# Output projection of the last unit placed before the other unit's MLP, with row shifts by small matrix products, in a one-core Perceiver-style kernel

## What is computed

```python
x = x + cross_attention(ctx, layernorm(x), mask)     # 16 heads of 64, keys from ctx
x = x + causal_attention(layernorm(x))               # one head of 256
x = x + ffn(layernorm(x))                            # two layers, below
```

```python
h = shift_token(x)                                   # right half of the features: from the row above
q, k, v = split(h @ wqkv)                            # 8 heads of 64
q, k = rotary(l2norm(q) * qs), rotary(l2norm(k) * ks)
x = x + local_attention(q, k, v) @ wo                # window of 128
h = layernorm(shift_token(x)) * lg + lb              # shift again, then mean and variance by row
a, g = split(h @ w1 + b1)
x = x + (a * gelu(g)) @ w2 + b2                      # hidden width 682
```

## Time and profile before

| | us |
|---|---|
| median of 3 runs | 1082.38 |
| lowest, highest | 1081.82, 1087.89 |
| the profiled execution | 1083.38 |
| its span in the profile | 1081.6 |

### The profile page before, as it was taken

One profiled execution on the slowest core, in us unless ns is written; L12 is line 12 of the kernel. 1 busy time (PEld: TensorE's weight loads), 2 busy tenths in 40 slices (PEclk: granted clock), 3 DMA queues, 4 the chain that ended last, 5 costly groups with the idle time before them and its releaser, 6 DMA issues. The chain is left out here.

```text
span 1081.6 us, 25643 instructions
## 1 busy us (share of the span) xinstructions
PE 1020.2 (94%) x8664; PEld 947.2 (88%) x8665; DVE 822.5 (76%) x3037; ACT 659.4 (61%) x1532; POOL 203.0 (19%) x260
## 2 busy tenths in 40 slices
PE   3899999999999999999999999978999999999976
PEld 3789999999999999999999998957788998989976
DVE  5897787786787786787786877679978988988642
ACT  4466566565566565566665565557667777757732
POOL 0011111111111111111111111540024212352222
PEclk9999999999999999999999998999999999999997
DMA  6000000000000000000000100600010000110001
GB/s 200 22 3 12 11 1 0 11 12 2 13 2 0 11 12 2 13 2 0 11 12 2 33 2 2 195 4 2 1 41 21 2 2 21 34 47 2 2 3 38
DMA packets 29458, 21.73 MB, mean 20 GB/s; under 512 B 13653, under 2 KB 26921, under 8 KB 29353
## 3 DMA queue, kind: packets, MB, share of 16 engines
q1 hardware_dynamic: 28368, 20.22, 6.4%
q10 hardware_dynamic: 984, 0.13, 0.2%
HBM read 19.23 MB, written 1.05 MB: 19 GB/s over the span
## 5 line engine op out<-in xcount | busy, mean ns | idle before, releaser
L295 PEld LDWEIGHTS pv_ps<-v,pt 128*128 128x128 f32 x1792 | 215.9, 193 | 8.8 <-issue 2.4
L295 PE MATMUL pv_ps<-v,pt 128*128 128x65 f32 x1792 | 216.3, 273 | 2.7 <-DVE o L820 1.4
L798 DVE CUSTOM_DVE_ANT_0 s_sb<-s_ps,pen,mstate 128x256 f32<-128x256 f32 (+1 forms) x512 | 199.8, 446 | 13.4 <-issue 10.5
L493 ACT ACTIVATE probs<-s_sb,mbias 128x256 f32<-128x256 f32 (+1 forms) x512 | 203.2, 470 | 0.0
L660 POOL TENSOR_TENSOR o<-o,alpha 128x260 f32<-128x260 f32 x128 | 85.6, 669 | 573.5 <-ACT alpha L487 573.5
L502 ACT ACTIVATE pt<-turn 128x512 f32<-128x512 f32 x128 | 76.3, 596 | 121.4 <-PE turn L282 107.4
L282 PE MATMUL turn<-ident,probs 128*128 128x128 f32 x896 | 123.9, 278 | 4.1 <-DVE ql L776 2.1
L282 PEld LDWEIGHTS turn<-ident,probs 128*128 128x128 f32 x896 | 98.7, 144 | 14.1 <-issue 2.6
L820 DVE TENSOR_TENSOR o<-o,pv_ps 128x260 f32<-128x260 f32 x128 | 53.9, 421 | 47.0 <-PE pv_ps L295 36.2
L271 PE MATMUL s_ps<-kh,qh 64*128 64x256 f32 (+1 forms) x512 | 79.4, 306 | 4.2 <-DVE kl L770 1.8
L770 DVE TENSOR_TENSOR kl<-proj,kh 128x512 fp32r<-128x512 f32 (+1 forms) x63 | 41.2, 654 | 51.7 <-ACT kh L480 51.4
(11 more groups left out here) (367 smaller groups left out, 2737.8 us busy)
## 6 DMA issues: line engine op xcount, KB each, us to landing
raw<-in_ctx SPq DMA_DIRECT2D x24, 128.0 KB, 2.1
f_wqkv_raw<-in_L_ffn_wqkv SPq DMA_DIRECT2D x6, 512.0 KB, 5.3
wkv_raw<-in_L_xattn_Wkv SPq DMA_DIRECT2D x2, 1024.0 KB, 8.1
f_w_raw<-in_L_ffn_w SPq DMA_DIRECT2D x8, 256.0 KB, 5.1
f_w_raw<-in_L_ffn_w SPq DMA_DIRECT2D x2, 640.0 KB
wq_raw<-in_L_xattn_Wq SPq DMA_DIRECT2D x1, 1024.0 KB, 8.1
wout_raw<-in_L_xattn_Wout SPq DMA_DIRECT2D x1, 1024.0 KB, 10.3
f_wo_raw<-in_L_ffn_wo SPq DMA_DIRECT2D x2, 512.0 KB, 4.7
```

The costliest lines, as they stand in the source:

```text
L295: last = pe.matmul(t.pv_ps[:, u, :], t.pt[g % 2][:, u, kt, :], t.v[:, kt, h, :], start=(kt == 0), stop=(kt == kts - 1))
L493: last = act.activation(t.probs[g % 2][:, u, 0:kts * P], t.s_sb[g % 2][:, u, 0:kts * P], ACT.Exp, bias=t.mbias[:, at:at + 1], scale=0.125)
L798: last = dve.tensor_tensor_reduce(out=t.s_sb[g % 2][:, u, 0:width], in0=t.s_ps[g % 2][:, u, 0:width], in1=t.pen[:, 0:width], scale=1.0, sc ...
```

## The change

It has two independent parts, both only an order of instructions and a few buffers.

**The tail.** All engines' loops end at T = 8 and the rest is written out. Unit 7 gets its own second buffer for the transposed output (`turned_outputs`, in `f_xt`, free by then), and its own banks (`f_s`, `f_turn`, free after the attention). Both `turn_output` and both `project_output` of unit 7 now stand ahead of `up(6,2)`. The two DMA pairs for unit 7 are replaced by products with a 128 x 384 matrix `f_rows` (zeros with an identity in the middle), written to `f_s`: four for the statistics (`last_stats`) and three for the moments (`last_moments`); DVE copies the results out. `up(7,0)` and `up(7,1)` go ahead of `down(6,0)`. `down(7,0)` waits block by block. `add_constants(7)` goes ahead of `hidden_lo(7,0)`. The last unit's rows are stored in two DMAs of 128 KB.

**The start.** On ACT the copies of unit 0's projections and its `squares` and `norms` are moved ahead of the high parts of `w12` and `w2`. On PE `mid_weighted(3)` goes behind `turn_latents(1)`; on DVE `mid_store_turned(3)` goes ahead of `rotate_sin(0,1)` and `mid_add(3)` further back.

```diff
+    def turned_outputs(u, q):
+        if u == LAST and q:
+            return [x[:, 0:4 * P].rearrange("p (k n) -> p k n", k=4) for x in t.xt]
+        return [o[:] for o in t.ot]
...
+            def last_stats(bank):
+                pe.wait_ge(s["tails"], UNITS)
+                down_one, from_above = t.rows[:, P - 1:2 * P - 1], t.rows[:, 2 * P - 1:3 * P - 1]
+                pe.matmul(bank[:, 0:6], down_one, t.tail_stats[:, 0, :], start=True, stop=False)
+                pe.matmul(bank[:, 0:6], t.ident[:], t.first_row[:], start=False, stop=True)
+                pe.matmul(bank[:, 6:12], down_one, t.tail_stats[:, 1, :], start=True, stop=False)
+                pe.matmul(bank[:, 6:12], from_above, t.tail_stats[:, 0, :], start=False, stop=True).then_inc(s["stats_shifted"], 32)
+            def last_moments(bank):
+                pe.wait_ge(s["mv_ready"], UNITS)
...
-            for T in range(0, UNITS + 3):
+            for T in range(0, UNITS + 1):
...
+            turn_output(LAST, 0, t.g[2])
+            turn_output(LAST, 1, t.s[0])
+            project_output(LAST, 0, t.s[1])
+            project_output(LAST, 1, t.turn[0])
+            up(LAST - 1, 2, t.g[2])
+            last_stats(t.s[0])
+            pe.wait_ge(s["gated"], count(6, LAST - 1, 0))
+            up(LAST - 1, 3, t.g[0])
+            pe.wait_ge(s["gated"], count(6, LAST - 1, 1))
+            up(LAST - 1, 4, t.g[1])
+            last_moments(t.s[0])
+            edge(LAST, t.turn[1])
+            pe.wait_ge(s["edge_read"], LAST + 1)
+            turn_normed(LAST, t.turn[1])
+            pe.wait_ge(s["gated"], count(6, LAST - 1, 2))
+            up(LAST - 1, 5, t.g[2])
+            pe.wait_ge(s["gated"], count(6, LAST - 1, 3))
+            up(LAST, 0, t.g[0])
+            pe.wait_ge(s["gated"], count(6, LAST - 1, 4))
+            up(LAST, 1, t.g[1])
...
+            down(LAST - 1, 0, t.s[0])
...
+            for k in range(2, HB):
+                pe.wait_ge(s["gated"], count(6, LAST - 1, 3 + k))
+                up(LAST, k, t.g[k % 3])
...
+                    if q == 0 and u == LAST:
+                        pe.wait_ge(s["u_ready"], count(6, u, m))
...
-            high_piece(act, s, ("w12", first["w12"]))
-            high_piece(act, s, ("w2", first["w2"]))
-            first_deviations(2, slice(QT, 2 * QT))
-            mid_exponentials(3)
             store_tile(0, 0, 0, t.g[0])
             store_tile(0, 0, 1, t.g[1])
             squares(0, 0)
+            mid_exponentials(3)
             store_tile(0, 0, 2, t.g[0])
+            first_deviations(2, slice(QT, 2 * QT))
             norms(0, 0)
             store_tile(0, 1, 0, t.g[1])
             store_tile(0, 1, 1, t.g[2])
             squares(0, 1)
+            high_piece(act, s, ("w12", first["w12"]))
+            high_piece(act, s, ("w2", first["w2"]))
```

More of the change, by code:

```diff
@@ L1212, in _ @@
             rows = out.rearrange("b (t p) d -> p (b t) d", p=P)
-            for u in range(B, UNITS):
+            for u in range(B, LAST):
                 tile = 2 * (u % B)
@@ L1216, in _ @@
                 sp.dma_start(rows[:, tile:tile + 2, :], t.y[:, tile:tile + 2, :]).then_inc(s["stored"], 16)
-            sp.wait_ge(s["stored"], 16 * B)
+            for q in range(QT):
+                sp.wait_ge(s["y_ready"], 8 + 2 * LAST + q + 1)
+                sp.dma_start(rows[:, TILES - QT + q, :], t.y[:, TILES - QT + q, :]).then_inc(s["stored"], 16)
+            sp.wait_ge(s["stored"], 16 * (B + 1))
         @block.gpsimd
@@ L1376, in project_output @@
                 for k in range(4):
-                    last = split_product(pe, bank[:, 0:D], [o[:, k, :] for o in t.ot], [w[:, k, :] for w in t.wo], k == 0, k == 3)
+                    last = split_product(pe, bank[:, 0:D], [o[:, k, :] for o in turned_outputs(u, q)], [w[:, k, :] for w in t.wo], k == 0, k == 3)
                 last.then_inc(s["e_done"], 1)
@@ L1638, in _ @@
                     mid_turn_probs(3)
-                    mid_weighted(3)
                 if valid(T - 2):
@@ L1914, in _ @@
                     squares(T + 1, 1)
+            output_hi(LAST, 1, t.s[0])
+            gelu(LAST - 1, 1, t.g[1])
+            hidden_hi(LAST - 1, 0)
+            hidden_hi(LAST - 1, 1)
+            deviations(LAST)
+            gelu(LAST - 1, 2, t.g[2])
+            gelu(LAST - 1, 3, t.g[0])
+            hidden_hi(LAST - 1, 2)
+            hidden_hi(LAST - 1, 3)
+            gelu(LAST - 1, 4, t.g[1])
+            wide_hi(LAST)
+            hidden_hi(LAST - 1, 4)
+            gelu(LAST - 1, 5, t.g[2])
+            hidden_hi(LAST - 1, 5)
+            for k in range(HB):
+                gelu(LAST, k, t.g[k % 3])
+                if k:
+                    hidden_hi(LAST, k - 1)
+            hidden_hi(LAST, HB - 1)
         @block.vector
```

106 lines of the change are left out of this document (85 added, 21 removed).

## The result

| | before | after |
|---|---|---|
| median, us | 1085.59 (6 runs) | 1075.21 (6 runs) |
| lowest, highest | 1081.82, 1087.89 | 1074.09, 1077.37 |
| the profiled execution, its span | 1083.38, 1081.6 | 1075.66, 1073.8 |

The ratio is 0.9908, with a 95% interval of 0.9887 to 0.9928. The change makes the kernel faster by 0.9%, 10.4 us by the medians; forecast were 12.7, and 1069.7 us. The forecast of 1069.7 started from 1082.38 us for the kernel before, the median of 3 runs; over these 6 runs it is 1085.59. So of the 5.5 us by which the time was missed, 3.2 are the kernel before and 2.3 the change. Span against span, 7.8 us are gained.

The account below looks back on a forecast made before the run. Tail bound by a chain over all engines and two DMA pairs, start by ACT and DVE; gains of 9.8 (tail) and 2.9 (start) sum to 12.7 us, taking the median from 1082.38 to 1069.7, range 1067.0 to 1074.5.

Parts of the forecast that it names:

- The tail: From unit 6's first gelu to the end: 7.8 us between gelus, 1.8 behind the last, 0.2 for the store; 9.8 us gained.
- the waits: PE's waits in the new tail: 1.0 for `f_ot`, 0.9 ahead of `turn_normed`, 1.5 ahead of `up(7,0)`; sum 3.4 us.
- The seven small products: Tail, f32 products on PE in place of the DMAs: 0.30 us each, 2.1 in all, bounds 1.5 and 2.7.
- the two gelus: Tail, from the gelu of unit 6's block 0 to that of unit 7's block 5: 31.6 us instead of 39.4.
- the halved store: Tail's end, the last unit's rows stored in two halves: 0.2 us gained, bounds 0 and 0.6.
- The clock in the tail: Rival: PE's clock falls in the new tail, doubling 20 to 35 matmuls, 2.0 to 3.5 us: about 1072.4; chance 0.26.
- The start: Start of the third stage: unit 1's projection at about 725.9 instead of 728.76; 2.9 us gained, bounds 0 and 5.0.
- POOL's low parts of those weights come later, but the MLP reads them over 50 us on: Start, POOL's low parts delayed by the moved high parts: their later making was given no cost.
- The mechanism of the copies: Start, ACT: four high parts (2.32 us) leave the place ahead of unit 0's copies; DVE's reduction starts 1.6 to 2.1 us earlier.
- The new memsets on POOL: Start, POOL: they lie ahead of its wait for the first weights and were taken to cost nothing.
- the start's lead is lost: Rival: in the start, DVE, 92% busy from 720 to 760, loses the lead; 1072.6 us, chance 0.13.

Follow-up runs that it names:

- start_back: The kernel before with the start's new order, but the high parts of `w12` and `w2` left where they were: 1081.54 us, ratio 0.9958.
- weights_back: The changed kernel with the high parts of `w12` and `w2` put back where they were before: 1072.03 us, ratio 0.9865.
- tail_late: tail_only with POOL's writes for the small products put behind the first layer's low parts: 1075.39 us, ratio 0.9896.
- back_late: weights_back with POOL's writes for the small products put behind the first layer's low parts: 1070.68 us, ratio 0.9854.
- consts_late: The changed kernel with POOL's writes for the small products put behind the first layer's low parts: 1074.78 us, ratio 0.9895.
- tail_only: The changed kernel with the start's orders on ACT, PE and DVE as in the kernel before: 1074.44 us, ratio 0.9887.
- after_split: The changed kernel with POOL making the low parts of `w12` and `w2` in short pieces of one row block: 1070.94 us, ratio 0.9862.
- no_low: The changed kernel with POOL writing zeros in place of the low parts of `w12` and `w2`: 1071.72 us, ratio 0.9865.

## Why the prediction was wrong, point by point

- **The number:** 3.2 of the missing 5.5 us are the kernel before, at 1085.59 and not 1082.38, which says nothing of the change. Taken from 1085.59, the forecast gain of 12.7 would give 1072.9; measured were 1075.21. The other 2.3 are, within 0.2, the 2.9 of the start, which did not come, less the 0.8 that the tail gave beyond its forecast. The range ended at 1074.5, 0.7 below the measured time; counted from 1085.59 it would have held it.
- **The tail**, forecast 9.8 us: right in its steps, and 0.8 short. Of the waits, 3.5 stand for 3.4. The seven small products were taken at 0.30 and cost 0.22 where they follow one another, 0.6 less in all, the lower bound; between the two gelus 0.3 of it is left (31.3 instead of 31.6). From the last addition (1071.25) to the end it is 2.55 us instead of 3.05 (3.0 in the other profiles with the whole store, 2.5 to 2.6 with the halved one): the halved store gave 0.5, not 0.2. The estimate of 0.3 by the Trainium skill's page DMA: Bandwidth & Descriptors (Anatomy of one DMA) was low as well. That section gives its figures for transfers that GpSimd issues, and this store is issued by SP.
- **The clock in the tail:** the rival with the chance of 0.26 didn't come. Behind the waits of 0.98, 0.97 and 1.57 the windows show 1.00. In the start it did fall, behind 2.13 and 2.93 us, which I had not given a price.
- **The start**, forecast 2.9 us earlier: this is the failed term. Unit 1's projection was to start at 725.9 and started at 730.80, 48.3 us after S instead of 45.66; start_only, the start's change by itself, has a ratio of 0.999 (0.9972 to 1.0007). The sentence that failed is "POOL's low parts of those weights come later, but the MLP reads them over 50 us on." I asked who reads what they write, and not what runs on DVE while they run. The mechanism of the copies was right: start_back has them alone and is 4.6 us faster by the medians and 1.8 by its marks, both inside my bounds of 0 to 5.0. The high parts on ACT were moved out of the way of these copies, together with 6.76 us of POOL's work, from around DVE's wait of 3.24 us into a stretch where DVE has none. The held instructions cost 0.35 + 0.70 + 2.25 = 3.3 us of DVE (L2034, L2038 and the pair). Their old place isn't free either once the copies come earlier (0.8 us in start_back), but the move gained nothing: start_back and weights_back keep the parts where they were and have P at 6.65 us behind the second sums.
- **"The new memsets on POOL … at nothing":** by the medians this cannot be told from nothing (tail_late, back_late, consts_late). In single profiles they move POOL's pause from 1.32 us at 700 to 2.14 at 697, and with it what `wo`'s low part holds: `f_mid_bias`, 1.93 us instead of 1.22.
- **The rival "the start's lead is lost"** named the right place and cited DVE's load, 36.77 of 40 us; its time of 1072.6 let the lead shrink to nothing, and by the medians that is what came. But its reason, that DVE has no room, is not what the rows show: DVE itself took 3.3 us longer.
- **The sum with what the runs showed:** tail_only times start_back is 0.9887 by 0.9958, 0.9845. weights_back and back_late, which have both, stand at 0.9865 and 0.9854. back_late has the lowest median of these kernels, 1070.68 us, 4.5 below the changed one; beside weights_back and after_split (1070.94) it is not told apart.

What stays open: P to U, 300 us of the loop that the change does not touch, varies from 299.7 to 304.3 us between profiles. It follows the time that PE spends at the lower clock in it: 299.7 us with 3 us of it (no_low), 300.6 to 301.5 with 7 (six profiles, the kernel before among them), 302.0 to 302.3 with 10 (four) and 303.1 to 304.3 with 14 (five). The other executions agree: of those of the kernel before beside start_back, those at a mean clock of 0.989 took 1080.94 to 1084.58 us, those at 0.978 to 0.980 1088.70 to 1092.80. Part of any comparison of single executions is this, the 3.4 us above among them. What makes the clock fall in one execution and not in the next I did not find.

## What to carry to other kernels

When work is moved in time, look up not only who reads its result but what the engines beside it do while it runs: an elementwise instruction on POOL that lasts 2 to 3 us belongs where DVE waits or works out of PSUM. And look again when DVE's own work moves: in start_back it ran into the parts that had not moved. Change the order of one engine at a time, or at least check that each moved block buys something; here two lines were moved for nothing, and cost 4.1 us where the whole change gained 10.4. And in a tail that is bound by a chain over several engines, try the order first (here 7.3 us with what belongs to it), and then cheaper steps (3.3).
